# Routing by batches, and rows sent home by number: a mixture-of-experts stage and the projections behind it on one Trainium2 core

## What is computed

```
logits = x @ gate_w.T + gate_b
probs = jax.nn.softmax(logits, axis=-1)
idx = jnp.argmax(probs, axis=-1)
top_prob = jnp.max(probs, axis=-1)
one_hot = jax.nn.one_hot(idx, E, dtype=jnp.int32)
pos = jnp.take_along_axis(jnp.cumsum(one_hot, axis=0), idx[:, None], axis=1)[:, 0] - 1
keep = pos < capacity
safe_pos = jnp.where(keep, pos, 0)
buf = buf.at[idx, safe_pos].add(x * keep[:, None].astype(x.dtype))
hdn = jax.nn.relu(jnp.einsum('ecd,edf->ecf', buf, w1) + b1[:, None, :])
eout = jnp.einsum('ecf,efd->ecd', hdn, w2) + b2[:, None, :]
out = eout[idx, safe_pos] * (top_prob * keep.astype(x.dtype))[:, None]
```

## Time and profile before

| | |
|---|---|
| three runs, median | 4310.81 us (4302.95 to 4311.17) |
| the profiled execution | 4302.39 us |
| its span, first to last instruction | 4300.5 us |
| granted TensorE clock, mean | 0.876 |
| PE, DVE, ACT, POOL busy | 3288.2, 3456.8, 2195.2, 2295.2 us |
| phase `b`, from the first load to the last sum | 2683.7 to 2952.7 us |
| phase `c_project` | 2953.3 to 3019.0 us |

### The profile page before, as it was taken

One profiled execution on the slowest core, in us unless ns is written; L12 is line 12 of the kernel. 1 busy time (PEld: TensorE's weight loads), 2 busy tenths in 40 slices (PEclk: granted clock), 3 DMA queues, 4 the chain that ended last, 5 costly groups with the idle time before them and its releaser, 6 DMA issues. The chain is left out here.

```text
span 4300.5 us, 114046 instructions
## 1 busy us (share of the span) xinstructions
PE 3288.2 (76%) x45981; PEld 2794.0 (65%) x45981; DVE 3456.8 (80%) x7351; ACT 2195.2 (51%) x5213; POOL 2295.2 (53%) x2836
## 2 busy tenths in 40 slices
PE   5767777777777777777777772373999979988998
PEld 3667777677777777777777772351666647765765
DVE  4799999999999999999999995304788878865885
ACT  3344444444444444444444442020788869946992
POOL 0566666767767666677676663114110038815870
PEclk9888898898888888888888885586999989998999
DMA  2110110111101101101011010312000001101110
GB/s 72 31 35 24 35 34 23 36 33 28 40 25 35 34 24 35 34 24 40 29 32 37 24 34 18 110 50 52 2 2 2 2 23 39 39 15 32 36 41 25
DMA packets 150011, 138.28 MB, mean 32 GB/s; under 512 B 65208, under 2 KB 101123, under 8 KB 149228
## 3 DMA queue, kind: packets, MB, share of 16 engines
q1 hardware_dynamic: 147436, 127.53, 10.9%
q0 software_dynamic: 2048, 3.45, 0.3%
HBM read 96.00 MB, written 14.69 MB: 26 GB/s over the span
## 5 line engine op out<-in xcount | busy, mean ns | idle before, releaser
L1014 DVE TENSOR_REDUCE banks<-a_tmp 128x64 f32<-128x64 f32 (+14 forms) x960 | 669.3, 697 | 33.1
L466 PE MATMUL banks<-a_xseg,a_w_k 128*128 128x128 f32 x2048 | 304.4, 321 | 163.0 <-DVE a_wx L1021 159.1
L466 PEld LDWEIGHTS banks<-a_xseg,a_w_k 128*128 128x128 f32 x2048 | 298.3, 237 | 169.5 <-DVE a_wx L1021 165.2
L466 PE MATMUL banks<-a_xseg,a_w_v 128*128 128x128 f32 x2048 | 305.5, 322 | 110.6 <-DVE a_wx L1021 109.2
L466 PEld LDWEIGHTS banks<-a_xseg,a_w_v 128*128 128x128 f32 x2048 | 299.4, 237 | 116.4 <-DVE a_wx L1021 114.8
L793 POOL TENSOR_TENSOR a_w<-a_wx,a_a 128x160 f32<-128x160 f32 (+5 forms) x384 | 288.6, 752 | 149.4 <-DVE a_wx L1021 149.3
L1012 DVE TENSOR_TENSOR a_tmp<-a_w,banks 128x64 f32<-128x64 f32 (+8 forms) x576 | 346.4, 601 | 25.5 <-DVE a_w L1021 0.5
L793 POOL TENSOR_TENSOR a_wx<-a_w,a_a 128x128 f32<-128x128 f32 (+5 forms) x384 | 262.6, 684 | 157.6 <-DVE a_w L1021 154.9
L539 PE MATMUL banks<-a_wm,a_kt 64*64 64x64 f32 x8192 | 256.8, 221 | 103.6 <-ACT a_wm L670 103.6
L1012 DVE TENSOR_TENSOR a_tmp<-a_wx,banks 128x320 f32<-128x320 f32 (+5 forms) x384 | 315.7, 822 | 14.0 <-DVE a_wx L1021 0.8
L778 POOL TENSOR_TENSOR a_st<-a_st,a_ab 128x512 f32<-128x512 f32 x256 | 325.9, 1273 | 0.0
(11 more groups left out here) (311 smaller groups left out, 9031.8 us busy)
## 6 DMA issues: line engine op xcount, KB each, us to landing
a_ab<-decays SPq DMA_DIRECT2D x512, 128.0 KB, 3.1
d_Vs<-d_V SPq DMA_DIRECT2D x128, 128.0 KB, 2.4
sent<-b_zero SPq DMA_DIRECT2D x1, 2560.0 KB, 10.7
b_xe<-sent SPq DMA_DIRECT2D x8, 320.0 KB, 3.6
back<-b_eo SPq DMA_DIRECT2D x8, 320.0 KB, 2.5
a_xseg<-xn SPq DMA_DIRECT2D x32, 70.0 KB, 3.1
xn<-a_xnT SPq DMA_DIRECT2D x8, 256.0 KB, 2.5
decays<-a_dc SPq DMA_DIRECT2D x128, 8.0 KB, 1.5
```

The lines of the kernel that those rows point to most:

```text
L466: t = e.matmul(b[:, m * SW:(m + 1) * SW].rearrange("p (b t) -> p b t", b=NB), self.wT[n][:, j, ct * P:(ct + 1) * P], xs[:, :, off:off + SE ...
L1014: e.tensor_reduce(sums[:, t - 1], prod, AX.X, ALU.add).then_inc(*step.at((g, t, "sum")))
```

## The change

In phase `b`, x is loaded by batch, and norm, rows, logits, choice, counts and slots are made batch by batch (`dve_norm`, `dve_choose`, `dve_slots`, `act_rows`, `pe_logits`, `pe_counts`). The rows are normalised on ACT instead of DVE. The gate's bias is added on DVE in the copy out of PSUM, and the matmuls of L1286 are gone. The first of equal logits is found with a rank table instead of seven running sums. Each batch's eight tiles are sent as soon as its slots are known. A row carries its token's number as a 129th element. POOL reads those numbers (`gps_place`) out of an expert's rows and scatters the expert's output straight to the token's row in `back`, five indirect transfers for each expert; there is no gather. `back` and `sent` are filled from one DRAM row (`nothing`, zeros and a number out of bounds) in two transfers that SP issues between `a_setup` and `a`; the fill in phase `b` is gone. All weights of C and D are loaded behind the experts' weights (`late`).

In `c_project`, class `Home` loads `back` by batch with plain transfers, DVE adds a batch to x and makes its norm, ACT makes the rows, and PE takes transposes, q, k and V for four tiles in turn.

```diff
+        for signal, key, dst, src in self.late:
+            e.dma_start(dst, src).then_inc(*signal.at(key))
         q.wait_ge(self.w_sent, NTILE - 1)
         rows = lambda a, x: a[x * CAPACITY:(x + 1) * CAPACITY, :].rearrange("(n p) d -> p n d", p=P)
+        for x in range(NE):
+            if x >= 4:
+                q.wait_ge(self.s_eturned, x - 4)
+                q.wait_ge(self.s_place, x - 4)
+            e.dma_start(self.xe[x % 4][:], rows(self.sent, x)).then_inc(*self.l_xe[x % 4].at(x))
+
...
+    def gps_place(self, e, q, x):
+        q.wait_ge(self.l_xe[x % 4], x)
+        if x >= 4:
+            q.wait_ge(self.w_eo[x % 2], (x - 4, CT - 1))
+        e.tensor_copy(self.place[x % 4][:], self.xe[x % 4][:, :, D]).then_inc(*self.s_place.at(x))
+
+    def gpsimd(self, e, q):
+        q.wait_ge(self.l_gate, "token")
+        e.tensor_copy(self.xn[:, :, D], self.token[:]).then_inc(*self.s_token.at())
+        q.wait_ge(self.s_token)
+        for signal, key in self.home.empty:
+            q.wait_ge(signal, key)
+        for b in range(NB):
+            q.wait_ge(self.s_index, b)
+            for g in range(b * TPB, (b + 1) * TPB):
+                e.indirect_dma_start(self.sent, bass.IndirectOffsetOnAxis(self.to[:, g:g + 1], 0), self.xn[:, g, :], None,
+                                     bounds_check=SLOTS - 1, oob_is_err=False).then_inc(*self.w_sent.at(g))
...
         for x in range(4):
-            e.dma_start(self.xe[x][:], rows(self.sent, x)).then_inc(*self.l_xe[x].at(x))
+            self.gps_place(e, q, x)
         for x in range(NE):
+            q.wait_ge(self.s_eo, x)
+            q.wait_ge(self.s_place, x)
+            for j in range(CT):
+                e.indirect_dma_start(self.back, bass.IndirectOffsetOnAxis(self.place[x % 4][:, j:j + 1], 0), self.eo[x % 2][:, j, :], None,
+                                     bounds_check=NT - 1, oob_is_err=False).then_inc(*self.w_eo[x % 2].at((x, j)))
             if x + 4 < NE:
-                q.wait_ge(self.s_eturned, x)
-                e.dma_start(self.xe[x % 4][:], rows(self.sent, x + 4)).then_inc(*self.l_xe[x % 4].at(x + 4))
-            q.wait_ge(self.s_eo, x)
-            e.dma_start(rows(self.back, x), self.eo[x % 2][:]).then_inc(*self.w_eo[x % 2].at(x))
-
-    def gpsimd(self, e, q):
-        q.wait_ge(self.w_zero)
-        q.wait_ge(self.s_index, "to")
-        for g in range(NTILE):
-            e.indirect_dma_start(self.sent, bass.IndirectOffsetOnAxis(self.to[:, g:g + 1], 0), self.xn[:, g, :], None,
-                                 bounds_check=SLOTS - 1, oob_is_err=False).then_inc(*self.w_sent.at(g))
-        q.wait_ge(self.s_index, "come")
+                self.gps_place(e, q, x + 4)
         for x in (NE - 2, NE - 1):
-            q.wait_ge(self.w_eo[x % 2], x)
-        for g in range(NTILE):
-            e.indirect_dma_start(self.rows[:, g, :], None, self.back, bass.IndirectOffsetOnAxis(self.come[:, g:g + 1], 0),
-                                 bounds_check=SLOTS - 1, oob_is_err=False).then_inc(*self.l_rows[g * GROUPS // NTILE].at(g))
+            q.wait_ge(self.w_eo[x % 2], (x, CT - 1))
+
...
+    def pe_logits(self, e, q, n):
+        c, b = self.c, n // 2
+        if n % 2 == 0 and b >= 2:
+            q.wait_ge(self.s_route, ("lg", b - 2))
+        q.wait_ge(self.l_gate, "token")
+        q.wait_ge(self.s_columns, n)
+        for j in range(4):
+            g = 4 * n + j
+            t = e.matmul(c.bank(2 + b % 2)[:, g * NE:(g + 1) * NE], self.xnT[n % 2][:, j * P:(j + 1) * P], self.gw[:], start=True, stop=True)
+        t.then_inc(*self.s_logits.at(n))
+
+    def pe_counts(self, e, q, b):
+        c, gs = self.c, slice(b * TPB, (b + 1) * TPB)
+        cols = slice(gs.start * NE, gs.stop * NE)
+        flat = self.oh[:, gs, :].rearrange("p g e -> p (g e)")
+        q.wait_ge(self.s_route, ("one", b))
+        if b:
+            q.wait_ge(self.s_route, ("pos", b - 1))
+        e.matmul(c.bank(4)[:, cols], self.cst["tri"][:], flat, start=True, stop=True)
+        e.matmul(c.bank(5)[:, cols], self.cst["ones"][:], flat, start=True, stop=True).then_inc(*self.s_counts.at(b))
+
     def tensor(self, e, q):
...
+    def dve_norm(self, e, q, b):
+        gs = slice(b * TPB, (b + 1) * TPB)
+        self.norm.batch(e, q, self.X, lambda q, b: q.wait_ge(self.x_loaded[b], "x"), b)
+        self.norm.ready(q, b)
+        e.scalar_tensor_tensor(self.minus[:, gs], self.norm.mv[:, gs, 0], -1.0, self.norm.rstd[:, gs], ALU.mult,
...
+    def dve_slots(self, e, q, b):
+
+        c, r, g0 = self.c, self.s_route, b * TPB
+        gs = slice(g0, g0 + TPB)
+        over_g = lambda a: a[:].rearrange("p (o e) -> p o e", o=1).broadcast_to([P, TPB, NE])
+        totals = lambda g: c.bank(5)[:, g * NE:(g + 1) * NE]
+        ranks = c.bank(4)[:, g0 * NE:(g0 + TPB) * NE].rearrange("p (g e) -> p g e", e=NE)
+        ex, eq, oh, pre, slot = self.ex, self.eq, self.oh, self.pre, self.slot
+        q.wait_ge(self.s_counts, b)
+        for g in range(g0, g0 + TPB):
+            if g:
+                q.wait_ge(r, ("base", g - 1))
+                e.tensor_tensor(self.base[:, g, :], self.base[:, g - 1, :], totals(g - 1), ALU.add).then_inc(*r.at(("base", g)))
+            else:
...
+        e.tensor_reduce(slot[:, gs], pre[:, gs], AX.X, ALU.add).then_inc(*r.at(("slot", b)))
+        q.wait_ge(r, ("slot", b))
+        e.tensor_copy(self.to[:, gs], slot[:, gs]).then_inc(*self.s_index.at(b))
...
+        c, r, gate = self.c, self.s_route, self.home.gate
+        for b in range(NB + 2):
+            if b < NB:
+                self.dve_norm(e, q, b)
+            if b >= 2:
+                self.dve_slots(e, q, b - 2)
+            if 1 <= b <= NB:
+                q.wait_ge(self.l_gate, "token")
+                self.dve_choose(e, q, b - 1)
...
+    def act_rows(self, e, q, n):
+        b = n // 2
+        q.wait_ge(self.x_loaded[b], "x")
+        q.wait_ge(self.s_minus, b)
+        for g in range(4 * n, 4 * n + 4):
+            e.activation(self.xn[:, g, 0:D], self.X[:, g, :], ACT.Identity, scale=self.norm.rstd[:, g:g + 1],
...
 
     def scalar(self, e, q):
         c = self.c
+        self.act_rows(e, q, 0)
         for n in range(NTILE // 4):
+            if n + 1 < NTILE // 4:
+                self.act_rows(e, q, n + 1)
             q.wait_ge(self.s_turned, n)
             if n >= 2:
...
+class Home:
...
+    def sync(self, e, q):
+        for b in range(NB):
+            g = slice(b * TPB, (b + 1) * TPB)
+            e.dma_start(self.rows[:, g, :], self.back[b * T:(b + 1) * T, :].rearrange("(n p) d -> p n d", p=P)).then_inc(*self.l_rows[b].at())
+
+    def add(self, e, q, b):
+        q.wait_ge(self.l_rows[b])
+        q.wait_ge(self.s_gate)
+        for g in range(b * TPB, (b + 1) * TPB):
+            e.scalar_tensor_tensor(self.X[:, g, :], self.rows[:, g, :], self.gate[:, g:g + 1], self.X[:, g, :], ALU.mult,
+                                   ALU.add).then_inc(*self.s_sum.at(g))
+
...
+    def pe_turn(self, e, q, n):
+        b = self.c.bank(n % 2)
+        if n >= 2:
+            q.wait_ge(self.s_columns, n - 2)
+        q.wait_ge(self.s_xn, 4 * n + 3)
+        for j in range(4):
+            t = e.transpose(b[:, j * P:(j + 1) * P], self.xn[n % 2][:, j, :], self.c.ident[:])
...
+        self.pe_turn(e, q, 0)
+        for n in range(last + 1):
+            if n < last:
+                self.pe_turn(e, q, n + 1)
+            self.pe_qk(e, q, n)
+            self.pe_v(e, q, n)
...
+    def dve_norm(self, e, q, b):
+        gs = slice(b * TPB, (b + 1) * TPB)
+        if self.home:
+            self.home.add(e, q, b)
+        self.norm.batch(e, q, self.X, lambda q, b: self.home and self.home.ready(q, b), b)
+        self.norm.ready(q, b)
+        e.scalar_tensor_tensor(self.minus[:, gs], self.norm.mv[:, gs, 0], -1.0, self.norm.rstd[:, gs], ALU.mult,
+                               ALU.mult).then_inc(*self.s_minus.at(b))
...
+        self.dve_norm(e, q, 0)
+        for b in range(NB):
+            if b + 1 < NB:
+                self.dve_norm(e, q, b + 1)
+            for i in range(4 * b, 4 * b + 4):
+                self.dve_rotate(e, q, i)
...
     def scalar(self, e, q):
-        self.cols.scalar(e, q)
-        for n in range(NTILE // 4):
+        last = NTILE // 4 - 1
+        self.act_rows(e, q, 0)
+        for n in range(last + 1):
+            q.wait_ge(self.s_turned, n)
+            e.activation(self.xnT[:, n * BANK:(n + 1) * BANK], self.c.bank(n % 2), ACT.Copy).then_inc(*self.s_columns.at(n))
+            if n < last:
+                self.act_rows(e, q, n + 1)
             q.wait_ge(self.s_v, n)
...
+    phase["nothing"] = np.where(np.arange(D + 1) < D, 0.0, NOBODY)[None, :]
...
-    sent, back = (dram(n, [SLOTS, D], "Internal") for n in ("sent", "back"))
+    sent, back = dram("sent", [SLOTS, D + 1], "Internal"), dram("back", [NT, D], "Internal")
...
+        empty = [(c.dma("s_sent_empty"), 0, sent, cd["nothing"].broadcast_to([SLOTS, D + 1])),
```

(20 more changed lines are left out.)

294 lines of the change are left out of this document (139 added, 155 removed).

## The result

The changed kernel takes 4391.26 us, the median of 4 runs (4387.49 to 4391.85), against 4310.99 (4302.95 to 4312.30) for the kernel before on the same chip. The ratio is 1.0188 with a 95% interval of 1.0171 to 1.0206: slower by 80 us, where 59 us less was forecast. Its profiled execution took 4391.85 us with a span of 4390.1, the one of before 4302.4 with 4300.5. One execution of `e2_many_dram_rows` further down was in a slower state (4510.75 us, at a granted clock of 0.73 where the others had 0.88) and is left out of every number here.

What follows compares the result with a forecast made beforehand. Phase `b`'s one-engine-at-a-time chain, experts between two strings of 32 POOL issues, was taken to delay the end. 20 - 47.4 + 0 - 42.0 + 18.4 = -51.0 us from 4302.4 gave 4251.4, put at 4252, range 4230 to 4286.

Steps and rivals of the forecast that it cites:

- part 1: Fill moved ahead of `a_xseg`: plus 20 us, nothing hiding it, with bounds of 14 and 47 us.
- Slower than before: Fill ahead of `a_xseg` takes 91 us, under 52 GB/s, all engines reading the same few hundred bytes; chance 0.06.
- The 516-byte rows: In the fill, rows of 516 bytes cost about 20 beats for 16, some 24 us instead of 19.4.
- Part 2: Routing by batches in phase `b` lets POOL finish sending earlier, at 2765.0 against 2812.4: minus 47.4 us.
- POOL held by DVE: In phase `b` POOL can't issue while DVE works, adding some 20 us, total 4271; chance 0.05.
- Part 3: Experts in phase `b`: PE sets 10.07 us an expert and POOL keeps up at about 8.5 us; change 0.
- Part 4: From the last expert's output to `c_project`: 8.3 us instead of 50.3, minus 42.0 us.
- phase wait of 0.6: Term of 0.6 us for the wait between the last scatter's landing and `c_project`, within the 8.3 us.
- Part 5: `c_project` takes 84 us, 65.7 before, plus 18.4; rounds of 8.9 us set by the order on ACT.
- Cold projections: In `c_project` gaps keep PE at the lower clock, 27 us more, total 4279; chance 0.13.

Runs made afterwards that it cites:

- e2_many_dram_rows: Changed kernel, both fills in the same place but read from a DRAM table of 5120 equal rows instead of one row: 4256.95 us, 0.9874 of before.
- e1_sbuf_source: Changed kernel, both fills in the same place but read from a 128-row SBUF tile: 4263.10 us, 0.9896 of before.
- e5_act_order: Changed kernel with the fill in pieces from SBUF in phase `a`; in `c_project` ACT makes next-round rows before V's copy: 4238.24 us, 0.9829 of before.

## Why the prediction was wrong

**The step that failed: part 1, "I take 20 us", and its upper bound of 47 us.** The fill cost 145.6 us. The sum is otherwise sound: 4251.4 + 125.6 for the fill + 9.9 for the setup - 2.7 - 0.1 + 5.8 - 0.8 + 2.6 for the other rows of the table gives 4391.7, and 4391.85 was measured. The value came from the row "with the same size of piece", a fill of as many rows of 512 bytes from SBUF. That was the wrong likeness: the size of the pieces agreed, the source didn't, and the source was the new thing. The upper bound did come from a transfer out of one DRAM row, but that row lasted a microsecond in a stream that also loaded other things, and I rounded 162 GB/s to 100 by judgement. A bound that the trace didn't hold was treated as one. The honest upper end was open, and the text nearly said so.

**The rival "Slower than before" happened**, with its mechanism as written (all engines read the same few hundred bytes, `a_xseg` late, the whole recurrence with it). Its turning point of 91 us was too high: by the prediction's own sum a fill of 20 + 59 = 79 us is back at the median of before, and by the table the stretches behind the fill gave 66 us, so that one of 66 us used the gain up. It had a chance of 0.06, and its rate of "under 52 GB/s" was 31. Nothing in the trace of before spoke for 0.06 over 0.3.

**The 516-byte rows.** The stretches of after show 17 ns a row of 516 bytes and 14.5 ns a row of 512. The Trainium skill (DMA: Bandwidth & Descriptors, How a descriptor splits into AXI transactions) has such rows cost more beats, and by that rule the trace agrees in direction. In size it doesn't: from SBUF, where no source row holds the packets up, the time of the 516-byte rows and the one in which mostly 512-byte rows went are these in `e1_sbuf_source`:

```profile
98.00:102.00 4.00, 0.00 (x0) 0.00 (x0) 0.00 (x0) 0.00 (x0) 0.00 (x0) 0.50 1.27 186
...
106.00:110.00 4.00, 0.00 (x0) 0.00 (x0) 0.00 (x0) 0.00 (x0) 0.00 (x0) 0.50 1.15 332
```

The prediction's estimate of 20 beats for 16 would be a quarter more time, and these are near twice. `sent` landed in 17.2 us there, for 10.7 in 512-byte rows in the kernel before. It was the small term beside a large one all the same: with it, the whole fill took 22.5 us.

**Part 2, minus 47.4: minus 50.1.** POOL's first send came 33.9 us after the phase's start for 88.0, 54 us earlier (53 forecast), with one hole of 4.16 us after eight issues (6 forecast), and the counts held DVE up twice, 5.40 us each. "POOL held by DVE" falls: all 32 issues took 0.97 to 1.21 us at a distance of 1.28, beside 16 us of DVE work. The Trainium skill (SBUF - State Buffer, SBUF: two separate sides) warns of that for operations in two-port modes; no run here shows such a stop.

**Part 3, nothing: -0.1 us.**

**Part 4, minus 42.0: minus 36.2.** The landing was right, the "phase wait of 0.6" was the mis-sized term. I read it from DVE's row at the start of `c_project`, which shows only how long DVE stood, not how long POOL's drain took. The 5.4 us between the last gather's issue and `c_project` contained it, and I took them for a landing. Without the drain the stretch from the start of the last issue to `c_project` is 2.4 us for 8.2, so the wait of 0.6 was one of 6.

**Part 5, plus 18.4: plus 17.6.** The size agreed, the cause only in part. I had every round at 8.9 us by the order on ACT and wrote that DVE "is not the bound". The trace has 17.1 us for two rounds, near twice 8.9. But `e5_act_order` takes the wait behind V's copy away and gains 9.3 us, 9.0 of them in the first round and the last two, and the middle keeps its pace: there DVE's sums and norm, 7.9 us in one block ahead of the products, would have set nearly the same period. Its 12.4 us of work in the 17.1 us of a batch (PE had 11.7) was indeed no bound, and its place in the order was. Two of the terms were low, eight sums at 2.2 us for 3.2 and four ACT rows at 1.3 for 1.6. PE's clock was 0.90 from the second batch on, so "Cold projections" falls.

## What to carry to other kernels

Don't fill memory from one DRAM row: from sixteen different rows or an SBUF tile the same 4.74 MB took 21 and 22.5 us for 147.8. A DMA share near 1 with a rate far below what the queue has shown elsewhere, and a share that falls while the rate stays, were the signs here that the packets stood in line for something outside the engines. When a copy is made faster by another source, count its packets before saying why: they can have changed too. And when a change brings a transfer of a kind that the trace doesn't have, its upper bound is open, and its place ahead of a load that everything waits for turns that into the risk of the whole change. A cost that comes back wherever you push it, like POOL's drain here, should be pushed to where its engine is idle, not away.

## What the runs showed of the hardware

- Reads of one DRAM row of 512 or 516 bytes were served at 29 to 36 GB/s, 14.5 to 17 ns each, at a DMA share of 1.01 as at one of 0.12. 4096 packets of 512 bytes took 59.3 us from one row, 19.9 from four, 8.0 from sixteen and 7.8 from 4096.
- A DRAM-to-DRAM transfer whose rows follow one another without a gap on both sides went in packets of several rows: 1280 for 5120 rows from a table of four, 320 from one of sixteen, 48 from one of 5120.
- From SBUF, packets of 516 bytes moved 167 to 186 GB/s with a DMA share of 1.23 to 1.27, and mostly 512-byte ones right behind them 332.
- Slow packets beside other work are not harmless: in 15 of the 16 segments with some 8 us of them TensorE stopped for 2 to 6 us in the middle of a run of products that wait for nothing (64.0 us), and in the stretch shown its clock was 0.50 behind it. In each stop one 16 KB packet of the instruction queue moved late. With 4 us of slow packets no time was lost.
- The first drain of POOL behind indirect DMAs cost some 6 us, also 84 us later, when they had long landed (6.27 us ahead of `c_qm` for 0.37).
